# Edges loaded and counted earlier, and head 0 aggregated ahead of head 1's last chunk, in a two-block graph attention kernel

## What is computed

```python
def gat_conv(x, src, dst, W, a_src, a_dst, b, heads, out_ch):
    h = (x @ W).reshape(n, heads, out_ch)
    alpha_src = jnp.einsum('nhc,hc->nh', h, a_src)
    alpha_dst = jnp.einsum('nhc,hc->nh', h, a_dst)
    e = leaky_relu(alpha_src[src] + alpha_dst[dst], 0.2)
    p = exp(e - segment_max(e, dst)[dst])
    alpha = p / segment_sum(p, dst)[dst]
    return segment_sum(h[src] * alpha[:, :, None], dst) + b   # heads side by side

def block0(x):                       # W1: 768 -> 8 heads x 768, W2: 6144 -> 768
    h = elu(gat_conv(x, src, dst, W1, ..., heads=8, out_ch=768))
    return gat_conv(h, src, dst, W2, ..., heads=1, out_ch=768)

def block1(x):                       # W1, Wr1: 768 -> 1024, W2, Wr2: 1024 -> 768
    h1 = relu(layer_norm(gat_conv(x, ..., heads=4, out_ch=256))) + (x @ Wr1 + br1)
    return layer_norm(gat_conv(h1, ..., heads=1, out_ch=768)) + (h1 @ Wr2 + br2)

x = layernorm(x + block0(x))
x = layernorm(x + block1(x))
```

## Time and profile before

| | |
|---|---|
| time, three runs | 353.0, 353.04, 353.94 us; median 353.04 |
| profiled execution | 353.03 us, of which 351.2 are the span from the first to the last instruction |
| TensorE | busy 343.7 us (98% of the span), 2049 matmuls |
| VectorE | busy 214.4 us (61%) |
| ScalarE | busy 219.0 us (62%) |
| GpSimd | busy 249.4 us (71%) |
| data | 65.95 MB, 188 GB/s in the mean |

### The profile page before, as it was taken

The page is one execution under the profiler, slowest core; times in us unless marked ns, Lnnn a source line. Parts: engine busy times, 40 slices in busy tenths (PEclk is TensorE's granted clock), DMA queues, the critical chain, the costliest instruction groups (busy, mean ns, idle before and its releaser), DMA issues.

```text
span 351.2 us, 6049 instructions
## 1 busy us (share of the span) xinstructions
PE 343.7 (98%) x2049; PEld 297.0 (85%) x2051; DVE 214.4 (61%) x543; ACT 219.0 (62%) x383; POOL 249.4 (71%) x165
## 2 busy tenths in 40 slices
PE   7999999999999999999999999999999999999994
PEld 4888989889988988988898898889777888888883
DVE  4999873354527327354541834464797899964776
ACT  5988597547736854773775486479585865444601
POOL 2479769576693965769397486959757899697911
PEclk9999999999999999999999999999999999999999
DMA  8887968475747547575754757654563557355002
GB/s 256 302 303 214 404 214 264 178 207 163 233 131 238 158 135 239 135 242 145 213 179 136 223 179 240 212 179 145 171 202 104 204 177 216 119 174 184 2 0 90
DMA packets 24833, 65.95 MB, mean 188 GB/s; under 512 B 1984, under 2 KB 3056, under 8 KB 24816
## 3 DMA queue, kind: packets, MB, share of 16 engines
q1 hardware_dynamic: 20880, 55.55, 48.6%
q10 hardware_dynamic: 3936, 10.18, 10.0%
HBM read 64.94 MB, written 0.79 MB: 187 GB/s over the span
## 4 chain that ended last, share of the span: by engine, by line
PE 93%; DVE 4%; DMA 1%; issue 0%; ACT 0%; DVEq 0%
PE ps L1098 65%; PE ps L1200 10%; PE ps L1495 10%; PE ps L1550 2%; PE ps L1166 2%; DMA x_sb<-in_x 1%; PE ps L1293 1%; PE ps L1151 1%; DVE stats L1944 1%; PE ps L1229 1%; DVE ps L2201 1%; PE ps L1434 1%; DVE z L2208 1%; PE ps L1573 0%; PE ps L1251 0%
## 5 line engine op out<-in xcount | busy, mean ns | idle before, releaser
L401 POOL TENSOR_TENSOR ring_lo<-raw,ring_hi 128x768 fp32r<-128x768 f32 x92 | 167.2, 1851 | 65.1 <-ACT ring_hi L388 65.0
L388 ACT ACTIVATE ring_hi<-raw 128x768 fp32r<-128x768 f32 x96 | 77.3, 839 | 33.8 <-PE ps L1098 28.5
L1098 PE MATMUL ps<-ring_hi,zT_hi 128*128 128x256 f32 (+1 forms) x256 | 69.8, 345 | 0.0
L1098 PE MATMUL ps<-ring_lo,zT_hi 128*128 128x256 f32 (+1 forms) x256 | 67.8, 338 | 0.0
L1098 PE MATMUL ps<-ring_hi,zT_lo 128*128 128x512 f32 (+1 forms) x256 | 67.5, 338 | 0.0
L417 POOL TENSOR_TENSOR ring_lo<-raw,ring_hi 128x512 fp32r<-128x512 f32 (+1 forms) x40 | 59.4, 1519 | 10.3 <-ACT ring_hi L410 10.3
L1712 DVE CUSTOM_DVE_ANT_0 e<-ps,att 128x768 f32<-128x768 f32 x36 | 32.4, 954 | 46.7 <-PE ps L1098 46.7
L1098 PE MATMUL ps<-ring_hi,xT_hi 128*128 128x512 f32 (+1 forms) x192 | 51.2, 340 | 0.0
L1098 PE MATMUL ps<-ring_hi,xT_lo 128*128 128x512 f32 (+1 forms) x192 | 50.7, 337 | 0.0
L1098 PE MATMUL ps<-ring_lo,xT_hi 128*128 128x512 f32 (+1 forms) x192 | 50.5, 337 | 0.0
L1098 PEld LDWEIGHTS ps<-ring_lo,zT_hi 128*128 128x128 f32 x256 | 43.3, 188 | 5.6
(11 more groups left out here) (193 smaller groups left out, 552.1 us busy)
## 6 DMA issues: line engine op xcount, KB each, us to landing
raw<-in_L_gnn_W SPq DMA_DIRECT2D x54, 768.0 KB, 4.5
raw<-in_L_gnn_Wr SPq DMA_DIRECT2D x8, 768.0 KB, 4.4
att<-in_L_gnn_a_src ACTq DMA_DIRECT2D x10, 384.0 KB, 3.9
att<-in_L_gnn_a_dst ACTq DMA_DIRECT2D x10, 384.0 KB, 4.9
raw<-in_L_gnn_W SPq DMA_DIRECT2D x4, 384.0 KB, 5.4
x_sb<-in_x SPq DMA_DIRECT2D x2, 256.0 KB, 5.2
rows_hc<-in_L_gnn_b SPq DMA_DIRECT2D x1, 512.0 KB, 7.3
rows_hc<-in_L_gnn_g SPq DMA_DIRECT2D x1, 512.0 KB, 8.1
```

Source lines behind the costliest of these rows:

```text
L388: eng.activation(slot_hi(c), raw_chunk(c), ACT.Copy).then_inc(hi_done, 1)
L401: eng.tensor_tensor(slot_lo(c), raw_chunk(c), slot_hi(c).bitcast(F32), ALU.subtract)\
L1098: last = pe.matmul(ps[:, at + to:at + to + hi - lo], a, b[:, lo:hi], start=start and n == 0 and to != D, stop=stop and n == PASSES - 1, sk ...
```

## The change

- SyncE issues the two edge loads ahead of chunk 0's two halves instead of behind them.
- VectorE converts the edges and makes its first five ramps first, ahead of chunk 0's low half and the first low half of x.
- TensorE counts the edges and makes head 0's scores before chunk 1 of phase 1 instead of chunk 2. The weights of head 0 are transposed in the middle of chunk 4, and head 0 is aggregated before chunk 5. The two clearing matmuls go; the first matmul of the product of z opens the bank itself (`opens`).
- ScalarE makes seven of the ramps before the copy of head 0's projection and three behind it; the splits of phase 1's chunks 2 and 3 come behind these.
- In head 0's ELU VectorE puts all four of head 1's dots, and the second low half of z, between the second and the third pair. ScalarE makes phase 2's chunks 4 and 5 and the copy of head 1's first tile behind the last exponential, ahead of the last high half of z.
- At the seam x1 is transposed in parts of two and four blocks instead of four and two, in other banks. The matmul of zeros goes. VectorE makes tile 0's low halves before it centres tile 1.

```diff
--- before.py
+++ after.py
@@ -220,8 +220,8 @@
         GAT2_NAT_AT = [2 * BANK, 0]
         GAT2_WT_AT = [3 * BANK + N, BANK + N]
         R2_AT = 4 * BANK
-        X1T_AT = [(3 * BANK, 2 * BANK), (5 * BANK, 6 * BANK)]
-        X1T_PARTS = [4, KD]
+        X1T_AT = [(2 * BANK, 3 * BANK), (6 * BANK, 5 * BANK)]
+        X1T_PARTS = [2, KD]
         H1_PART = KH // 2
         ELU_AT = [2 * BANK, 6 * BANK, 7 * BANK]
         AM_AT = [T_AT, S_AT + N]
@@ -603,10 +603,10 @@
                 sp.dma_start(x_sb[:, :, cols], x.rearrange("(t p) c -> p t c", p=P)[:, :, cols])\
                   .then_inc(x_loaded[b], 16)
 
+            sp.dma_start(edges[:, 0, :], src.rearrange("(p t) -> p t", p=P)).then_inc(edges_loaded, 16)
+            sp.dma_start(edges[:, 1, :], dst.rearrange("(p t) -> p t", p=P)).then_inc(edges_loaded, 16)
             sp.dma_start(raw[:, 0, 0:D], w1[:, 0, 0, :]).then_inc(single_loaded[0], 16)
             sp.dma_start(raw[:, 0, D:2 * D], w1[:, 1, 0, :]).then_inc(raw_full[0], 16)
-            sp.dma_start(edges[:, 0, :], src.rearrange("(p t) -> p t", p=P)).then_inc(edges_loaded, 16)
-            sp.dma_start(edges[:, 1, :], dst.rearrange("(p t) -> p t", p=P)).then_inc(edges_loaded, 16)
             load_x(1)
             sp.dma_start(raw[:, 1, 0:D], w1[:, 2, 0, :]).then_inc(single_loaded[1], 16)
             load_x(2)
@@ -925,12 +925,10 @@
 
             for c in (0, 1):
                 split_hi(act, 1, c)
-            steps(10, 14)
+            steps(10, 17)
             projected_hi(0)
-            for c in (2, 3):
-                split_hi(act, 1, c)
-            steps(14, ACT_STEPS)
-            for c in (4, 5):
+            steps(17, ACT_STEPS)
+            for c in (2, 3, 4, 5):
                 split_hi(act, 1, c)
             act.wait_ge(counted, 1)
             act.activation(step_sums, ps[:, STEPS_AT:STEPS_AT + 1 + N], ACT.Copy).then_inc(sums_copied, 1)
@@ -952,10 +950,13 @@
                 split_hi(act, 2, c)
             weights_hi(0)
             act.wait_ge(b1_ready, 2)
-            elu(0, between=lambda: projected_after_dots(1, 0))
-            split_hi(act, 2, 4)
+            def behind_last_exp():
+                for c in (4, 5):
+                    split_hi(act, 2, c)
+                projected_after_dots(1, 0)
+
+            elu(0, between=behind_last_exp)
             leaks(1)
-            split_hi(act, 2, 5)
             projected_after_dots(1, 1)
             exps(1, (1, 0))
             after_exps(1)
@@ -1088,7 +1089,7 @@
             def pieces(i):
                 return ((0, BANK, 0), (BANK, D, BANK)) if i == 0 else ((0, N, D), (N, D, 2 * BANK))
 
-            def product(at, i, lhs_hi, lhs_lo, w_hi, w_lo, start, stop, piece=None, passes=ALL):
+            def product(at, i, lhs_hi, lhs_lo, w_hi, w_lo, start, stop, piece=None, passes=ALL, opens=False):
 
                 last = None
                 for n, (a, b) in enumerate(three(lhs_hi, lhs_lo, w_hi, w_lo)):
@@ -1096,7 +1097,7 @@
                         continue
                     for lo, hi, to in pieces(i) if piece is None else pieces(i)[piece:piece + 1]:
                         last = pe.matmul(ps[:, at + to:at + to + hi - lo], a, b[:, lo:hi],
-                                         start=start and n == 0 and to != D,
+                                         start=n == 0 and (opens or start and to != D),
                                          stop=stop and n == PASSES - 1, skip_group_check=True)
                 return last
 
@@ -1294,28 +1295,22 @@
                 last.then_inc(counted, 1)
 
             for c in range(CH):
-                if c == 2:
+                if c == 1:
                     pe.wait_ge(b1_ready, 2)
                     count_edges()
                     scores(0)
-                project_chunk(1, 1, c, between=(lambda: weights(0)) if c == CH - 1 else None)
-
-            def clear_acc(b):
-                pe.matmul(ps[:, ACC + b * BANK:ACC + (b + 1) * BANK], zeros[:, 0:P], zeros[:, :],
-                          start=True, stop=False, skip_group_check=True)
-
-            aggregate_T(0)
-            clear_acc(1)
-            clear_acc(2)
-
-            def first_accumulate(c, i, passes=ALL, piece=None, start=False):
+                if c == CH - 1:
+                    aggregate_T(0)
+                project_chunk(1, 1, c, between=(lambda: weights(0)) if c == CH - 2 else None)
+
+            def first_accumulate(c, i, passes=ALL, piece=None, start=False, opens=False):
                 return product(ACC, i, node_tile(zT_hi, c, i), node_tile(zT_lo, c, i), slot_hi(c), slot_lo(c),
-                               start, False, passes=passes, piece=piece)
+                               start, False, passes=passes, piece=piece, opens=opens)
 
             pe.wait_ge(z_hi_done, 1)
             for c in (0, 1):
                 chunk(2, c)
-                first_accumulate(c, 1, passes=FIRST_TWO)
+                first_accumulate(c, 1, passes=FIRST_TWO, opens=c == 0)
             pe.wait_ge(z_lo_done, 1)
             for c in (0, 1):
                 first_accumulate(c, 1, passes=LAST_ONE)
@@ -1481,7 +1476,6 @@
                         last.then_inc(x1T_ps, 1)
 
             transpose_x1(0)
-            keep_warm(1, PROJ)
 
             def wide_product(q, at, i, passes=ALL):
 
@@ -1521,7 +1515,7 @@
                 wide_product(q, 0, 0, passes=LAST_ONE)
             for i in range(NT):
                 for q in w1a[2:] if i == 0 else w1a:
-                    if i == 0 and q["k"] == X1T_PARTS[0]:
+                    if i == 0 and q["k"] == BANK // P:
                         transpose_x1(1)
                     if q["k"] == X1T_PARTS[0] or i == 1 and q["k"] == 0:
                         pe.wait_ge(x1T_lo_done, 2 * i + 1 + (q["k"] > 0))
@@ -1656,8 +1650,6 @@
                     dve.tensor_scalar(hot(t), iota_ps[:, 1:1 + P], row_of[:, t:t + 1], weight_of[:, t:t + 1], ALU.is_equal, ALU.mult)\
                        .then_inc(hot_done, 1)
 
-            split_lo(dve, FIRST_PHASE, 0)
-            input_lo(0)
             dve.wait_ge(edges_loaded, 32)
             dve.tensor_copy(edges_f[:, :, :], edges[:, :, :]).then_inc(edges_cast, 1)
             dve.wait_ge(edges_cast, 1)
@@ -1674,10 +1666,12 @@
                     dve.tensor_scalar(step(t), numbers, edges_f[:, 0, t:t + 1], weight_of[:, t:t + 1],
                                       ALU.is_lt if t >= BELOW_FROM else ALU.is_ge, ALU.mult).then_inc(step_dve_done, 1)
 
-            split_lo(dve, FIRST_PHASE, 1)
             dve.wait_ge(iota_cast, 2)
             dve.wait_ge(edges_split, 5)
             late_steps(ACT_STEPS, ACT_STEPS + STEPS_EARLY)
+            split_lo(dve, FIRST_PHASE, 0)
+            input_lo(0)
+            split_lo(dve, FIRST_PHASE, 1)
             split_lo(dve, FIRST_PHASE, 2)
             input_lo(1)
             late_steps(ACT_STEPS + STEPS_EARLY, ET - STEPS_LAST)
@@ -1846,9 +1840,9 @@
             def elu(h, between=None):
 
                 for q in range(3):
-                    if q == 1 and between is not None:
+                    if q == 2 and between is not None:
                         between()
-                    if q >= 1:
+                    elif q >= 1:
                         elu_lo(h, q - 1)
                     dve.wait_ge(elu_exp, 3 * h + q + 1)
                     for c in range(2):
@@ -1909,10 +1903,14 @@
             normalised(FIRST_HEAD, (0, 1))
             projected_lo(0, 1)
             weights_lo(0)
-            dve.wait_ge(att_loaded, 32 * 2)
-            dots(1, a_s, 0, a_src_done)
-            dots(1, a_d, 1, a_dst_done, tiles=(0,))
-            elu(0, between=lambda: dots(1, a_d, 1, a_dst_done, tiles=(1,)))
+            def next_dots():
+                dve.wait_ge(att_loaded, 32 * 2)
+                dots(1, a_s, 0, a_src_done, tiles=(0,))
+                elu_lo(0, 1)
+                dots(1, a_s, 0, a_src_done, tiles=(1,))
+                dots(1, a_d, 1, a_dst_done)
+
+            elu(0, between=next_dots)
             dve.wait_ge(z_lo_done, 3)
             leaky_scores(1)
             for i in (1, 0):
@@ -2037,9 +2035,9 @@
             y_centre(0)
             y_piece(1, 0)
             y_piece(1, 1)
-            y_centre(1)
             x1_lo(0, 0)
             x1_lo(0, 1)
+            y_centre(1)
             y_stats(0)
             y_stats(1)
             x1_lo(1, 0)
```

## The result

Slower: 355.03 us median of 17 executions (353.88 to 356.56), against 353.36 us (352.53 to 354.84) for the kernel before beside it; ratio 1.004, 95% interval 1.0027 to 1.0053. The prediction was 352.9, with 351.7 to 353.9 as its range.

A forecast was written before the change was run, and what follows sets the result against it. TensorE, holding 93% of the last-ending chain, was taken as the bound. Terms: z's product 0.25 us later, head 1 0.1 later, seam 0.5 sooner, together -0.15 from 353.04: 352.9 us, range 351.7 to 353.9.

The forecast's parts named there:

- Before the count: Opening loads and VectorE's early work: early edges let VectorE finish chunk 2's low half some 0.8 us sooner (0.3 to 2.1).
- later loads keep their places: SyncE's queue at the start: the number of loads stays, so loads after the first four are not displaced.
- the new stop: TensorE at the transposes of head 0's weights: wants them at 33.75, waits for VectorE until about 34.5, 0.75 us.
- signs of being wrong: Transposes reached without a stop, TensorE's first product moved over 0.5 us, or the seam giving less than 0.3.
- count them as in time: ScalarE's last three ramps, now behind the projection's copy: assumed no delay, being used in the count's second half.
- Rival 2: Chunk 0 lands at 5.64, its whole issue delay late; VectorE gains only 0.3; 353.4 us, chance 0.13.
- rule on turns between queues: DMA engines alternate between queues packet by packet; chunk 0 would keep its 4.0 us, land at 5.64, sum 0.5 higher.
- Rival 1: VectorE gains 1.8 us or more, chunk 2's high half being no wall; no stop at the transposes; 352.1 us, chance 0.22.
- Rival 3: Head 1's softmax becomes the bound; slower from a 0.35 us stop at its transposes; 354.3 us with 1.5, chance 0.10.
- The edge cast: VectorE's opening conversion of the edges: expected at about 3.7 us, when their second load lands.
- the closed hole at z: TensorE ahead of z's product: the 0.48 us wait for z's high half goes, product starting at about 42.4.
- the seam: TensorE entering the second block: products 0.9 us after x1's first transpose, 0.5 us gained (0.3 to 0.7).

The follow-up runs named there:

- the first profile: Profiled execution of the changed kernel's own measurement, the longest of its 17: 356.56 us, span 354.8.
- start alone: Kernel before with only the change's SyncE load order and VectorE opening order; counting stays at chunk 2: 353.19 us, ratio 1.0004.
- splits early: Changed kernel with ScalarE's splits of phase 1's chunks 2 and 3 ahead of its last three ramps: 353.73 us, ratio 1.0011.
- both moves: Changed kernel, copy of head 0's transposed weights ahead of ScalarE's phase 2 splits, head 0's first low half behind the normalisation; output invalid: 353.20 us, ratio 0.999.
- the second profile: Changed kernel profiled again, unchanged: that execution took 354.17 us, span 352.4; median 354.38 us, ratio 1.0045 to the kernel before.
- the five matmuls of zeros: Changed kernel with five matmuls of zeros instead of one between the first transposes of x and the first product: 354.83 us, ratio 1.0038.
- The version that gained here: Seam of the change, start of before, head 0 aggregated between chunk 5's tiles, weights' copy first, VectorE's three ramps ahead of GpSimd's low halves: 351.31 us, ratio 0.9931.
- the start undone: Changed kernel with SyncE's load order and VectorE's opening order put back to those of before: 354.20 us, ratio 1.002.

## Why the prediction was wrong

**The step that failed** is in "Before the count": "The gain is 10.24 - 9.4, some 0.8 us", with 0.3 as its lower bound. VectorE lost 0.28 us there. The wall was seen rightly (chunk 2's low half waits for ScalarE's high half, after 0.97 us of idle, as forecast); what was wrong is when ScalarE gets there. I moved chunk 0's first half past the two edge loads and costed its landing (5.2; it was 5.64, the upper bound, and 5.95 in the first profile), and forgot the second load, chunk 1, which moves past the same two. It lands at 7.71, ScalarE waits 0.68 us for it, and the high half of chunk 2 starts at 9.66 where I had 8.54. In three of the eight profiles with the new start (start alone, splits early, both moves) ScalarE did not wait for chunk 1; there chunk 0's lateness alone, or chunk 2's own load (0.30 and 0.49 us of wait), put that high half at 9.12 to 9.53. So "later loads keep their places" did not keep their landings. In all eight VectorE's low half of chunk 2 starts between 10.00 and 10.79, in five with the loads and VectorE's order of before between 10.24 and 10.72: the forecast gain is not there.

**What follows from it.** The arithmetic on the counts starts at 28.76 instead of 27.76, the normalised weights end at 34.56 + 0.88 = 35.44 instead of 34.47, and the new stop is 1.27 us instead of 0.75. With TensorE itself 0.58 us later at the count, z's product stands 1.45 us behind before where I had 0.25: 0.97 of these 1.2 us are VectorE's, the rest lies between the transposes and z (8.09 us instead of 7.90). That TensorE's own delay would be hidden in the stop was right: with both waits taken away the two starts lie only 0.12 us apart at z. One of the signs of being wrong came half true: the first product moved by 0.44 us in the second profile and 0.74 in the first, against a bound of 0.5.

**A wait not priced.** This is the second step that failed: the 5.79 us from the transposes to the end of the aggregation were taken from before, with the copy of the transposed weights in time. The splits moved behind ScalarE's ramps free GpSimd, GpSimd frees the buffer, and the load for phase 2's chunks 2 and 3 is late. In the second profile the copy of the weights starts at 36.39, just as the splits end, and TensorE's 1.48 us of before become 1.62, against 1.54 in the runs without this wait; with the five matmuls of zeros they became 2.03. In three profiles with a half-paced first chunk it is a stop of 1.3 to 1.6 us. The prediction followed the ramps ("count them as in time") but not the splits behind them. By the medians this wait weighs no less than VectorE's: the changed kernel took 354.38 us and 353.85 with this wait alone gone, on one chip; the version with five matmuls 354.83 and the one with the splits early 353.73, on another; with VectorE's wait alone gone nothing was gained. The intervals of the ratios overlap, so how the loss divides between the two is not settled.

**Rivals.** Rival 2, chunk 0 late by its whole issue delay, is half of the mechanism that came about (chunk 1 is the other), at 4.0 us from issue to landing in the second profile. It fell short in its price, 353.4, since it kept a gain of 0.3 for VectorE and had no wait for the load. In the eight profiles with the new start chunk 0 lands between 5.51 and 5.95. The outcome of the Trainium skill's rule on turns between queues ("DMA: Bandwidth & Descriptors", Queues, rings and completion order), 5.64, agrees with the second profile to the digit; the first, at 5.95 and 4.3 us from its issue, lies beyond it. Rival 1 is refuted. Rival 3's place is there (0.30 us at head 1's transposes, and 11.19 us from z's product where I had 10.95), below its point of 0.35.

**What held.** The edge cast (3.7, measured 3.80), the closed hole at z, no bracket at x1 and its product 0.91 us after the transposes; the seam gave 0.63 us at the second tile where 0.5 was forecast. In sum, in the second profile and against -0.15 forecast: z 1.45, head 1 0.34, seam -0.63, and 0.06 between: 1.22, and its span is 1.2 longer.

**Open.** Why some executions run chunk 0 at half pace. It comes with both starts, and filling the hole moved no median. Also open is why the medians (355.03 to 353.36, and 354.38 to 353.00) lie somewhat further apart than the 1.2 us that the second profile explains; a longer wait for the load in other executions would do it, but was not shown.

## What to carry to other kernels

When a load moves behind others, cost the landing of every load that moves with it, and follow the engine that waits for the last of them; work that leaves one engine's busy stretch is worth only what the wall behind it lets through. When an order brings TensorE's demand forward, list all that must be ready at the new moment, the copy and the load behind the copy too: one wait removed can uncover the next. The version that gained here placed the dependent step between two halves of independent work and relieved the slow engine first; whether that placement alone pays was not run.

## What the hardware showed that I had not expected

- **VectorE beside GpSimd.** Three bf16 ramps took 3.94 us while GpSimd worked on a low half, 0.86 without. "SBUF — State Buffer" of the Trainium skill (Who interferes with whom) says that a VectorE operation in a two-port mode and a GpSimd one contend for a shared pair of ports, and that the one which issues first holds it for its whole instruction while the other is blocked. That these ramps run in such a mode no row shows; the times agree, as the ramps end at 11.73 + 3.94 = 15.67, 0.08 us after GpSimd's second low half (11.90 + 3.69). The ramps read from PSUM right behind (four in 1.90 us) take as long as in the kernel before.
- **A small load waits with the large ones.** 16 KB of edges landed 2.2 and 2.6 us after their issue when first on SyncE's queue, 5.3 and 5.4 us when behind x on ScalarE's, issued only 0.5 us later. The first third of x, with the same place and issue, went from 4.6 to 2.9 us when chunk 0 stood behind the edges.
- **Pace and granted clock.** In the changed kernel's first profile the granted clock is 0.50 from 8 to 10 us, the lower of its two levels (1.2 GHz). In the profile of the start undone it reads 1.00, while only four matmuls run in a microsecond where eight do in the changed kernel's second profile. The columns are the window and its length; the busy time and count of PE, PEld, DVE, ACT and POOL; then the granted clock, the share of the DMA engines and GB/s:

```profile
8.00:9.00 1.00, 1.00 (x4) 0.81 (x4) 0.96 (x7) 0.80 (x2) 0.00 (x0) 1.00 1.06 400
```
